# Expert tiles: the first product in three pieces of 512 columns instead of four of 384, and one of two projection pieces' rests made on GpSimd

## The chip, the cores and the metric

The kernel runs on one core of one Trainium2 chip. A core has a matrix engine (TensorE, PE), a vector engine (VectorE, DVE), a scalar engine (ScalarE, ACT), GpSimd (POOL) and a DMA-issuing engine (SyncE, SP), each with its own instruction queue; they meet through semaphores. The metric is the device time of one execution in microseconds, as the median of several executions.

## What is computed

A two-layer perceiver block over 16 x 64 tokens of width 512: cosine attention to a context, self-attention, a mixture of experts, cross-attention, a decayed attention and a feed-forward layer. The change is in the mixture of experts alone:

```python
scores = jax.nn.softmax(xf @ w_gate, axis=-1)
weights, idx = jax.lax.top_k(scores, TOP_K)            # 2 of 8 experts a token
...
h = jnp.einsum('ecd,edf->ecf', exp_x, c_fc)            # 512 -> 1536
a, g = jnp.split(h, 2, axis=-1)
h = jax.nn.silu(a) * g                                 # 768
exp_out = jnp.einsum('ecf,efd->ecd', h, c_proj)        # 768 -> 512
```

## The kernel before

`expert_layer` first routes: each of the 1024 tokens goes to two experts, the routed tokens are padded per expert to tiles of 128, and there are always ET = 23 such tiles. Then come 23 steps, one for each tile, written by `steps` as steps 0 and 1, a hardware loop over pairs of steps, and step 22.

Products are made of split operands, because TensorE multiplies the short type fp32r: each operand is a first part, which ScalarE makes by a copy into fp32r, and a rest, which VectorE makes by subtracting the first part from the whole (`rest`, L1049). Three products stand for one (first by first, first by rest, rest by first). Weights are split again for every tile: `fw` holds the two parts of the 512 x 1536 first weights, `pw` those of the 768 x 512 projection, each in one buffer only. `raw_fc` and `raw_pj` hold the whole weights of two experts; SyncE reloads one when the last tile that needs it has been split.

The order of the work is written out by hand, one function `step` for each engine, and each engine takes its instructions strictly in that order:

- TensorE (L950): `hidden(s, 0)` and `hidden(s, 1)` (12 matmuls of 384 columns each, into PSUM banks 0 and 1, the half under the silu), `turn_h(s - 1)` (6 transposes of the gated hidden values), `hidden(s, 2)` and `hidden(s, 3)` (the other half), `turn_x(s + 1)` (4 transposes of the next tile), `out_proj(s - 1)` (18 matmuls of 512 columns). `hidden(s, c)` waits for both parts of the tile (`x_lo`), for both parts of piece c of the weights (`fc_lo`), and until its bank was read.
- ScalarE (L1005): takes the result of two steps ago (`y_take`), then the first part of projection half 0, `silu(s, 0)`, `first_fc(s + 1, 0)`, `silu(s, 1)`, first parts of the turned hidden values (`first_h`, twice), of projection half 1, of piece 1 of the next tile's weights, of the next tile (`first_x`), of pieces 2 and 3. Ahead of `first_pj(s - 1, 0)` and of `first_fc(s + 1, 0)` its sequencer loads two values from memory (`parity_of`, `loaded`), which tell where the expert's weights lie and whether they have landed.
- VectorE (L1077): rest of projection half 0, of piece 0 of the next weights, of the turned hidden values (twice), of projection half 1; the gate product `product(s, 0)`, rest of piece 1, `product(s, 1)`, rest of the next tile (`rest_x`), rests of pieces 2 and 3.
- GpSimd (L1122): only issues DMAs: a tile's load, and the store of the tile two behind.

`first_fc(s + 1, c)` may not write `fw` before `hidden(s, c)` has read it:

```python
if not is_(s, 0):
    act.wait_ge(f_mm, BASE + 4 * s + c - 3)
nc.scalar.activation(fw[0][:, :, fc_cols(c)], raw_fc_of(par, c), ACT.Copy).then_inc(fc_hi, 1)
```

## Time and profile before

| | us |
|---|---|
| median of 3 runs | 2177.83 (2176.89 to 2182.11) |
| the profiled execution's own time | 2178.88 |
| its span from first to last instruction | 2177.1 |
| expert steps 1 to 21 in it, from the first matmul of step 1 to that of step 22 | 286.34 |

The span is a serial chain of six layers; the expert steps are its stretch from about 394 to 720 us. A row of the timeline gives start and duration in us, engine, line, operation, and in brackets how long the engine had been idle and what ended that. PE is TensorE's matmuls; L109 is the helper that issues split products; L1049 is the helper that makes rests.

### The profile page before, as it was taken

The page shows a single profiled execution, that of the slowest core. Times are in us where ns is not written, and L with a number is a line of the kernel's source. Part 1 is how long each engine was busy: PE and PEld are TensorE (multiplying, and loading weights), DVE is VectorE, ACT ScalarE, POOL GpSimd, SP SyncE. Part 2 cuts the span into 40 slices and gives each one's busy share as a digit, 9 for nine tenths or more (in the row PEclk, how much of TensorE's full clock was granted, in tenths as well). Part 3 has the DMA queues.
Part 4 walks back from the last instruction along what each step waited for, and adds up shares of the span by engine and source line. Part 5 has one row for each costly group of instructions (what it writes and reads, how often), then busy time and mean ns, then how long its engine had stood idle before and what let it go on. Part 6 is the DMA issues. An engine that isn't in the chain of part 4 may idle for free. (4 is left out here: it accounts for less than half of the span.)

```text
span 2177.1 us, 31504 instructions
## 1 busy us (share of the span) xinstructions
PE 1943.0 (89%) x10442; PEld 1494.0 (69%) x10442; DVE 1338.7 (61%) x2423; ACT 1120.6 (51%) x1846; POOL 125.4 (6%) x159
## 2 busy tenths in 40 slices
PE   7978983699999499999999999999968989858998
PEld 5647873699999477777777777787747666623443
DVE  5765662699998264536362635354448999839851
ACT  5753320688887244535353535444436666626640
POOL 0000002100000110000000000000000000012220
PEclk9989885899999799999999999999988888779999
DMA  7410005235332421001000101012040000020000
GB/s 262 147 54 1 0 0 222 112 131 205 130 150 89 153 68 49 34 29 34 29 34 29 48 14 48 14 48 92 1 171 1 1 1 1 1 82 0 5 10 25
DMA packets 25896, 137.45 MB, mean 63 GB/s; under 512 B 4066, under 2 KB 4194, under 8 KB 22116
## 3 DMA queue, kind: packets, MB, share of 16 engines
q1 hardware_dynamic: 19588, 116.18, 14.6%
q0 software_dynamic: 6240, 20.45, 2.8%
q8 instruction: 32, 0.52, 0.1%
q14 instruction: 36, 0.29, 0.0%
HBM read 116.17 MB, written 20.45 MB: 63 GB/s over the span
## 5 line engine op out<-in xcount | busy, mean ns | idle before, releaser
L109 PE MATMUL PS<-cT,qs 128*128 128x512 f32 x1152 | 295.6, 402 | 9.0 <-ACT pb L1406 7.0
L109 PE MATMUL PS<-pT,cN 128*128 128x512 f32 x1152 | 270.0, 392 | 1.7 <-DVE pT L1501 1.7
L109 PEld LDWEIGHTS PS<-cT,qs 128*128 128x128 f32 x1152 | 209.3, 189 | 59.9 <-issue 15.1
L109 PEld LDWEIGHTS PS<-pT,cN 128*128 128x128 f32 x1152 | 213.9, 188 | 45.3 <-DVE pT L1501 1.9
L109 PE MATMUL PS<-fw,xgT 128*128 128x384 f32 x1104 | 204.0, 339 | 3.0 <-DVE xgT L1049 3.0
L109 PEld LDWEIGHTS PS<-fw,xgT 128*128 128x128 f32 x1104 | 191.6, 189 | 8.3 <-issue 3.9
L109 PE MATMUL PS<-ws,xT 128*128 128x512 f32 x672 | 182.3, 430 | 6.4 <-DVE ws L563 4.9
L1049 DVE TENSOR_TENSOR fw<-W,fw 128x1536 fp32r<-128x1536 f32 x92 | 159.4, 1755 | 44.9 <-ACT fw L972 44.9
L1496 DVE TENSOR_REDUCE nmax<-PS 128x1 f32<-128x512 f32 x128 | 87.7, 685 | 156.9 <-PE PS L109 156.3
L109 PEld LDWEIGHTS PS<-ws,xT 128*128 128x128 f32 x672 | 138.8, 209 | 46.4 <-issue 11.3
L972 ACT ACTIVATE fw<-W 128x1536 fp32r x92 | 134.2, 1485 | 50.3 <-issue 50.3
L1401 ACT ACTIVATE qp<-PS 128x512 f32<-128x512 f32 x96 | 57.4, 598 | 189.6 <-PE PS L109 189.6
L2109 PE MATMUL PS<-xT,W 128*128 128x512 f32 x256 | 118.8, 614 | 1.3 <-ACT xT L2145 0.8
L1501 DVE TENSOR_TENSOR pT<-PS,pT 128x512 fp32r<-128x512 f32 x128 | 87.0, 685 | 52.9 <-ACT pT L1423 52.9
L2119 PE MATMUL PS<-W,hs 128*128 128x512 f32 x256 | 112.5, 592 | 0.0
L1423 ACT ACTIVATE pT<-PS 128x512 fp32r<-128x512 f32 x128 | 75.7, 598 | 65.4 <-PE PS L1301 65.2
L946 PE MATMUL PS<-pw,hT 128*128 128x512 f32 x414 | 101.8, 400 | 4.7 <-DVE hT L1049 4.7
L1406 ACT ACTIVATE pb<-PS,nmax 128x512 f32<-128x512 f32 x128 | 87.6, 685 | 34.5 <-DVE nmax L1496 34.4
L155 PE MATMUL PS<-cn,xn 128*128 128x128 f32 x160 | 29.0, 311 | 84.6 <-DVE xn L148 75.6
L1713 PEld LDWEIGHTS PS<-cn,W 128*128 128x128 f32 x512 | 78.0, 225 | 37.2 <-DVE W L2025 29.4
L142 POOL TENSOR_TENSOR rs<-ve,cn 128x1 f32<-128x1 f32 x41 | 23.4, 571 | 1390.2 <-DVE ve L137 1390.2
L1713 PE MATMUL PS<-cn,W 128*128 128x16 f32 x512 | 76.9, 285 | 22.5 <-DVE W L2025 22.4
(246 smaller groups left out, 3407.9 us busy)
## 6 DMA issues: line engine op xcount, KB each, us to landing
W<-in_fc SPq DMA_DIRECT2D x8, 3072.0 KB
cT<-in_ctxT SPq DMA_DIRECT2D x16, 768.0 KB, 5.4
raw_pj<-in_proj SPq DMA_DIRECT2D x8, 1536.0 KB, 6.4
ct_in<-in_ctxT SPq DMA_DIRECT2D x16, 768.0 KB
cn_in<-in_ctxN SPq DMA_DIRECT2D x16, 768.0 KB
W<-in_w SPq DMA_DIRECT2D x2, 4096.0 KB, 13.1
routed_x<-zero SPq DMA_DIRECT2D x23, 256.0 KB, 5.4
xg<-routed_x POOLq DMA_DIRECT2D x23, 256.0 KB, 3.2
```

The lines of the kernel that those rows point to most:

```text
L109: mm = nc.tensor.matmul(out, lhs(m, s), rhs(n, s), start=(opens and (s, m, n) == terms[0]), stop=((s, m, n) == terms[-1]))
L946: mm = nc.tensor.matmul(ps[7], hT[m][:, f, :], pw[n][:, f, :], start=(f == 0 and m == n), stop=(f == FK - 1 and m == 1))
L972: nc.scalar.activation(fw[0][:, :, fc_cols(c)], raw_fc_of(par, c), ACT.Copy).then_inc(fc_hi, 1)
L1049: return nc.vector.tensor_tensor(out, whole, first.bitcast(F32), ALU.subtract)
L1401: nc.scalar.activation(out, src, ACT.Copy, scale=scale).then_inc(w_sb, count)
L1406: nc.scalar.activation(pb[:, g % 2, :], ps[g % 2], ACT.Exp, bias=nmax[:, g % 4:g % 4 + 1], accum_out=rsum[:, g % 4:g % 4 + 1]).then_inc(e_ ...
L1423: nc.scalar.activation(turned(pT[0], g), ps[2 + g % 2].rearrange("p (j n) -> p j n", j=JK), ACT.Copy).then_inc(pt_hi, 1)
L1496: nc.vector.tensor_reduce(nmax[:, g % 4:g % 4 + 1], ps[g % 2], AX.X, ALU.max, negate=True).then_inc(m_dve, 1)
L1501: return nc.vector.tensor_tensor(out, whole, first.bitcast(F32), ALU.subtract)
L1713: mm = nc.tensor.matmul(ps[6 + c % 2][:, col:col + B], rb[:, t % RB, k * P:(k + 1) * P], sel, start=True, stop=True)
L2109: mm = nc.tensor.matmul(ps[n % HB], w16[:, k, f * P:(f + 1) * P], xT[g][:, k, :], start=(k == 0), stop=(k == DK - 1))
L2119: mm = nc.tensor.matmul(ps[HB + t % ZB], hs[:, t // TG, f, (t % TG) * P:(t % TG + 1) * P], w26[:, f, :], start=(f == 0), stop=(f == FT - 1))
```

## The change

The first product is cut into three pieces of 512 columns (12 matmuls each) instead of four of 384. Piece 0 holds columns 0 to 511 of the silu half; piece 1 holds its last 256 columns and the first 256 of the other half; piece 2 the remaining 512. So `silu` works on 512 and then 256 columns, and `product` on 256 and then 512, both after both silus. The rest of projection half 0 moves from VectorE to GpSimd, which gets its own semaphore for it, and stands there between the store of one tile and the load of a later one. VectorE's load of the parity for half 1 moves to just ahead of it.

```diff
@@ -669,7 +669,8 @@
         xg_in = [sem("xg_in3_0", pool_dma=True), sem("xg_in3_1", pool_dma=True)]
         y_out = [sem("y_out3_0", pool_dma=True), sem("y_out3_1", pool_dma=True)]
         x_mm, x_hi, x_lo = sem("x_mm3"), sem("x_hi3"), sem("x_lo3")
-        fc_hi, fc_lo, pj_hi, pj_lo = sem("fc_hi3"), sem("fc_lo3"), sem("pj_hi3"), sem("pj_lo3")
+        fc_hi, fc_lo, pj_hi = sem("fc_hi3"), sem("fc_lo3"), sem("pj_hi3")
+        pj_lo = [sem("pj_lo3_0"), sem("pj_lo3_1")]
         f_mm, silu_sb, hid_sb = sem("f_mm3"), sem("silu_sb3"), sem("hid_sb3")
         hT_mm, hT_hi, hT_lo = sem("hT_mm3"), sem("hT_hi3"), sem("hT_lo3")
         y_mm, y_sb = sem("y_mm3"), sem("y_sb3")
@@ -871,7 +872,9 @@
             return isinstance(s, int) and s == n
 
         def fc_cols(c):
-            return slice(c * HFE, (c + 1) * HFE)
+            return slice(c * 512, (c + 1) * 512)
+
+        MIX = 1024 - FE
 
         def pj_rows(g):
             return slice(g * HF, (g + 1) * HF)
@@ -895,14 +898,15 @@
                     end = sp.value_load(edge[0:1, ex - 2:ex - 1], min_val=0, max_val=ET)
                     u = ex % 2
                     sp.wait_ge(s_fc, BASE + 16 * ex)
-                    sp.wait_ge(fc_lo, end * 4 + BASE)
+                    sp.wait_ge(fc_lo, end * 3 + BASE)
                     sp.dma_start(raw_fc[:, u], a["fc"][ex]).then_inc(s_fc, 16)
                     sp.wait_ge(s_pj, BASE + 16 * ex)
-                    sp.wait_ge(pj_lo, end * 2 + BASE)
+                    for g in range(2):
+                        sp.wait_ge(pj_lo[g], end + BASE)
                     sp.dma_start(raw_pj[:, u], a["proj"][ex]).then_inc(s_pj, 16)
                 sp.wait_ge(s_fc, BASE + 16 * NE)
                 sp.wait_ge(s_pj, BASE + 16 * NE)
-                sp.wait_ge(fc_lo, BASE + 4 * ET)
+                sp.wait_ge(fc_lo, BASE + 3 * ET)
                 for dst, name in ((e.wq4, "wq4"), (e.wk4, "wk4"), (e.wv4, "wv4"), (e.wo4, "wo4")):
                     sp.dma_start(dst, a[name]).then_inc(e.s_w4, 16)
 
@@ -919,17 +923,20 @@
                 def hidden(s, c):
 
                     pe.wait_ge(x_lo, BASE + s + 1)
-                    pe.wait_ge(fc_lo, BASE + 4 * s + c + 1)
+                    pe.wait_ge(fc_lo, BASE + 3 * s + c + 1)
                     if not is_(s, 0):
-                        pe.wait_ge(silu_sb if c < 2 else hid_sb, BASE + 2 * s + c % 2 - 1)
-                    split_product(nc, ps[c][:, 0:HFE], lambda part, k: xgT[part][:, k, :],
+                        if c < 2:
+                            pe.wait_ge(silu_sb, BASE + 2 * s + c - 1)
+                        if c:
+                            pe.wait_ge(hid_sb, BASE + 2 * s + c - 2)
+                    split_product(nc, ps[c], lambda part, k: xgT[part][:, k, :],
                                   lambda part, k: fw[part][:, k, fc_cols(c)], DK).then_inc(f_mm, 1)
 
                 def turn_h(s):
 
                     pe.wait_ge(hT_lo, BASE + 2 * s)
+                    pe.wait_ge(hid_sb, BASE + 2 * s + 2)
                     for g in range(2):
-                        pe.wait_ge(hid_sb, BASE + 2 * s + g + 1)
                         for f in range(HF):
                             tr = nc.tensor.transpose(ps[5 + g][:, f * P:(f + 1) * P],
                                                      hid[:, (g * HF + f) * P:(g * HF + f + 1) * P], ident)
@@ -940,7 +947,7 @@
                     pe.wait_ge(y_sb, BASE + s)
                     for g in range(2):
                         pe.wait_ge(hT_lo, BASE + 2 * s + g + 1)
-                        pe.wait_ge(pj_lo, BASE + 2 * s + g + 1)
+                        pe.wait_ge(pj_lo[g], BASE + s + 1)
                         for f in range(g * HF, (g + 1) * HF):
                             for m, n in ((0, 0), (0, 1), (1, 0)):
                                 mm = nc.tensor.matmul(ps[7], hT[m][:, f, :], pw[n][:, f, :],
@@ -953,7 +960,6 @@
                     if not is_(s, 0):
                         turn_h(s - 1)
                     hidden(s, 2)
-                    hidden(s, 3)
                     if not is_(s, ET - 1):
                         turn_x(s + 1, 1 - u, pair + u)
                     if not is_(s, 0):
@@ -968,7 +974,7 @@
             def _(act):
                 def first_fc(s, c, par):
                     if not is_(s, 0):
-                        act.wait_ge(f_mm, BASE + 4 * s + c - 3)
+                        act.wait_ge(f_mm, BASE + 3 * s + c - 2)
                     nc.scalar.activation(fw[0][:, :, fc_cols(c)], raw_fc_of(par, c), ACT.Copy).then_inc(fc_hi, 1)
 
                 def first_pj(s, g, par):
@@ -981,14 +987,15 @@
 
                 def first_x(s):
                     act.wait_ge(x_mm, BASE + s + 1)
-                    act.wait_ge(f_mm, BASE + 4 * s)
+                    act.wait_ge(f_mm, BASE + 3 * s)
                     nc.scalar.activation(xgT[0][:, :, :].rearrange("p k t -> p (k t)"), ps[4], ACT.Copy).then_inc(x_hi, 1)
 
                 def silu(s, c):
-                    act.wait_ge(f_mm, BASE + 4 * s + c + 1)
+                    act.wait_ge(f_mm, BASE + 3 * s + c + 1)
                     if not is_(s, 0):
-                        act.wait_ge(hid_sb, BASE + 2 * s + c - 1)
-                    nc.scalar.activation(gated[:, fc_cols(c)], ps[c][:, 0:HFE], ACT.Silu).then_inc(silu_sb, 1)
+                        act.wait_ge(hid_sb, BASE + 2 * s)
+                    n = FE - 512 if c else 512
+                    nc.scalar.activation(gated[:, c * 512:c * 512 + n], ps[c][:, 0:n], ACT.Silu).then_inc(silu_sb, 1)
 
                 def first_h(s, g):
                     act.wait_ge(hT_mm, BASE + 2 * s + g + 1)
@@ -1024,13 +1031,12 @@
                         first_fc(s + 1, 1, par)
                         first_x(s + 1)
                         first_fc(s + 1, 2, par)
-                        first_fc(s + 1, 3, par)
 
                 par = parity_of(act, 0)
                 loaded(0, s_fc)
                 first_fc(0, 0, par)
                 first_x(0)
-                for c in range(1, 4):
+                for c in range(1, 3):
                     first_fc(0, c, par)
                 steps(act, step)
                 y_take(ET - 2, 1, (ET - 2) // 2)
@@ -1049,12 +1055,12 @@
                     return nc.vector.tensor_tensor(out, whole, first.bitcast(F32), ALU.subtract)
 
                 def rest_fc(s, c, par):
-                    ve.wait_ge(fc_hi, BASE + 4 * s + c + 1)
+                    ve.wait_ge(fc_hi, BASE + 3 * s + c + 1)
                     rest(fw[1][:, :, fc_cols(c)], raw_fc_of(par, c), fw[0][:, :, fc_cols(c)]).then_inc(fc_lo, 1)
 
                 def rest_pj(s, g, par):
                     ve.wait_ge(pj_hi, BASE + 2 * s + g + 1)
-                    rest(pw[1][:, pj_rows(g), :], raw_pj_of(par, g), pw[0][:, pj_rows(g), :]).then_inc(pj_lo, 1)
+                    rest(pw[1][:, pj_rows(g), :], raw_pj_of(par, g), pw[0][:, pj_rows(g), :]).then_inc(pj_lo[g], 1)
 
                 def rest_x(s):
                     ve.wait_ge(x_hi, BASE + s + 1)
@@ -1067,25 +1073,23 @@
                     rest(lo, ps[5 + g][:, 0:HF * P], hi).then_inc(hT_lo, 1)
 
                 def product(s, c):
-                    ve.wait_ge(silu_sb, BASE + 2 * s + c + 1)
-                    ve.wait_ge(f_mm, BASE + 4 * s + c + 3)
+                    ve.wait_ge(silu_sb, BASE + 2 * s + 2)
+                    ve.wait_ge(f_mm, BASE + 3 * s + c + 2)
                     if not is_(s, 0):
-                        ve.wait_ge(hT_mm, BASE + 2 * s + c - 1)
-                    nc.vector.tensor_tensor(hid[:, fc_cols(c)], gated[:, fc_cols(c)], ps[2 + c][:, 0:HFE],
-                                            ALU.mult).then_inc(hid_sb, 1)
+                        ve.wait_ge(hT_mm, BASE + 2 * s)
+                    cols = slice(MIX, FE) if c else slice(0, MIX)
+                    gate_in = ps[2] if c else ps[1][:, 512 - MIX:512]
+                    nc.vector.tensor_tensor(hid[:, cols], gated[:, cols], gate_in, ALU.mult).then_inc(hid_sb, 1)
 
                 def step(s, u, pair):
                     first, last = is_(s, 0), is_(s, ET - 1)
-                    if not first:
-                        par_p = parity_of(ve, s - 1)
-                        rest_pj(s - 1, 0, par_p)
                     if not last:
                         par = parity_of(ve, s + 1)
                         rest_fc(s + 1, 0, par)
                     if not first:
                         rest_h(s - 1, 0)
                         rest_h(s - 1, 1)
-                        rest_pj(s - 1, 1, par_p)
+                        rest_pj(s - 1, 1, parity_of(ve, s - 1))
                     product(s, 0)
                     if not last:
                         rest_fc(s + 1, 1, par)
@@ -1093,16 +1097,14 @@
                     if not last:
                         rest_x(s + 1)
                         rest_fc(s + 1, 2, par)
-                        rest_fc(s + 1, 3, par)
 
                 par = parity_of(ve, 0)
                 rest_fc(0, 0, par)
                 rest_x(0)
-                for c in range(1, 4):
+                for c in range(1, 3):
                     rest_fc(0, c, par)
                 steps(ve, step)
                 par = parity_of(ve, ET - 1)
-                rest_pj(ET - 1, 0, par)
                 rest_h(ET - 1, 0)
                 rest_h(ET - 1, 1)
                 rest_pj(ET - 1, 1, par)
@@ -1119,13 +1121,24 @@
                     pool.wait_ge(y_sb, BASE + s + 1)
                     nc.gpsimd.dma_start(yg_d[s * P:(s + 1) * P, :], y[:, s % 2, :]).then_inc(y_out[s % 2], 16)
 
+                def rest_pj(s):
+
+                    par = parity_of(pool, s)
+                    pool.wait_ge(pj_hi, BASE + 2 * s + 1)
+                    nc.gpsimd.tensor_tensor(pw[1][:, pj_rows(0), :], raw_pj_of(par, 0),
+                                            pw[0][:, pj_rows(0), :].bitcast(F32), ALU.subtract).then_inc(pj_lo[0], 1)
+
                 for s in range(ET):
                     if s >= 2:
                         pool.wait_ge(x_mm, BASE + s - 1)
                     nc.gpsimd.dma_start(xg[:, s % 2, :], xg_d[s * P:(s + 1) * P, :]).then_inc(xg_in[s % 2], 16)
+                    if s >= 3:
+                        store(s - 3)
                     if s >= 2:
-                        store(s - 2)
-                store(ET - 2)
+                        rest_pj(s - 2)
+                for s in range(ET - 3, ET - 1):
+                    store(s)
+                    rest_pj(s + 1)
                 store(ET - 1)
                 for u in range(2):
                     pool.wait_ge(y_out[u], 16 * ((ET + 1 - u) // 2))
```

On VectorE the two listings below show step 1, the second tile: from the rest of projection half 0 (`pw`, before) or of piece 0 of the next weights (`fw`, after) on. `fw` are rests of weight pieces, `hT` of turned hidden values, `pw` of projection halves, `hid` gate products, `xgT` the rest of the next tile; TENSOR_LOAD reads the parity. Before:

```order
L1049 ISA
L1049 TENSOR_TENSOR pw<-raw_pj,pw 128x1536
L889 TENSOR_LOAD parity
L889 ISA x2
L1049 ISA
L1049 TENSOR_TENSOR fw<-W,fw 128x4x384
L1049 TENSOR_TENSOR hT<-PS,hT 128x384 x2
L1049 ISA
L1049 TENSOR_TENSOR pw<-raw_pj,pw 128x1536
L1074 TENSOR_TENSOR hid<-gated,PS 128x384
L1049 ISA
L1049 TENSOR_TENSOR fw<-W,fw 128x4x384
```

After, the same step:

```order
L1055 TENSOR_TENSOR fw<-W,fw 128x4x512
L1055 TENSOR_TENSOR hT<-PS,hT 128x384 x2
L892 TENSOR_LOAD parity
L892 ISA x2
L1055 ISA
L1055 TENSOR_TENSOR pw<-raw_pj,pw 128x1536
L1082 TENSOR_TENSOR hid<-gated,PS 128x256
L1055 ISA
L1055 TENSOR_TENSOR fw<-W,fw 128x4x512
L1082 TENSOR_TENSOR hid<-gated,PS 128x512
L1055 TENSOR_TENSOR xgT<-PS,xgT 128x512
```

The first `pw` is gone from the head of the step; all that followed it keeps its order, with pieces of 4 x 512 in place of 4 x 384.

On GpSimd the listings show the stretch after the first three tile loads (`xg<-routed_x`). Before:

```order
L1125 DMA xg<-routed_x 128x512 x3
L1120 DMA routed_y<-y 128x512
L1125 DMA xg<-routed_x 128x512
L1120 DMA routed_y<-y 128x512
L1125 DMA xg<-routed_x 128x512
```

After:

```order
L1134 DMA xg<-routed_x 128x512 x3
L892 TENSOR_LOAD parity
L892 ISA x2
L1128 ISA
L1128 TENSOR_TENSOR pw<-raw_pj,pw 128x1536
L1134 DMA xg<-routed_x 128x512
L1122 DMA routed_y<-y 128x512
L892 TENSOR_LOAD parity
L892 ISA x2
L1128 ISA
L1128 TENSOR_TENSOR pw<-raw_pj,pw 128x1536
L1134 DMA xg<-routed_x 128x512
```

A subtraction (`pw`) stands ahead of every later tile load, and each store (`routed_y`) comes one tile load later than before.

## Rows read from the trace of the kernel before

**Rows 1.** The page: busy time of each engine over the whole span.
```profile
PE 1943.0 (89%) x10442; PEld 1494.0 (69%) x10442; DVE 1338.7 (61%) x2423; ACT 1120.6 (51%) x1846; POOL 125.4 (6%) x159
```

**Rows 2.** Windows, expert tiles 1 to 21: length, busy of each engine, granted clock, DMA.
```profile
core 0: us, PE busy (x) PEld busy (x) DVE busy (x) ACT busy (x) POOL busy (x), PEclk, DMA share, GB/s
409.27:695.61 286.34, 286.32 (x1596) 266.49 (x1597) 265.76 (x232) 236.20 (x253) 21.46 (x40) 1.00 0.37 136
```

**Rows 3.** Timeline of one tile, step 11: start, duration, engine, line, op, idle before.
```profile
559.34 4.43 PE L109 MATMUL PS<-fw,xgT 128*128 128x384 f32 x24
559.58 0.60 ACT L1003 ACTIVATE y<-PS 128x512 f32<-128x512 f32 x1 [0.77 <-PE PS L946]
...
561.05 1.49 ACT L976 ACTIVATE pw<-raw_pj 128x1536 fp32r x1 [0.87 <-issue]
562.45 0.47 ACT L991 ACTIVATE gated<-PS 128x384 f32<-128x384 f32 x1
562.69 1.76 DVE L1049 TENSOR_TENSOR pw<-raw_pj,pw 128x1536 fp32r<-128x1536 f32 x1 [0.25 <-ACT pw L976]
563.42 1.49 ACT L972 ACTIVATE fw<-W 128x1536 fp32r x1 [0.51 <-issue]
...
565.05 1.76 DVE L1049 TENSOR_TENSOR fw<-W,fw 128x1536 fp32r<-128x1536 f32 x1 [0.61 <-ACT fw L972]
...
566.73 1.01 DVE L1049 TENSOR_TENSOR hT<-PS,hT 128x384 fp32r<-128x384 f32 x2
...
567.66 1.75 DVE L1049 TENSOR_TENSOR pw<-raw_pj,pw 128x1536 fp32r<-128x1536 f32 x1
...
568.78 4.36 PE L946 MATMUL PS<-pw,hT 128*128 128x512 f32 x18
...
569.33 0.55 DVE L1074 TENSOR_TENSOR hid<-gated,PS 128x384 f32<-128x384 f32 x1
...
569.79 1.75 DVE L1049 TENSOR_TENSOR fw<-W,fw 128x1536 fp32r<-128x1536 f32 x1
571.46 0.55 DVE L1074 TENSOR_TENSOR hid<-gated,PS 128x384 f32<-128x384 f32 x1
571.92 0.68 DVE L1049 TENSOR_TENSOR xgT<-PS,xgT 128x512 fp32r<-128x512 f32 x1
...
572.98 1.23 PE L109 MATMUL PS<-fw,xgT 128*128 128x384 f32 x6
```

**Rows 4.** Groups by line, other shapes: count, busy, mean ns of one, idle before.
```profile
L597 DVE TENSOR_TENSOR sc<-PS,mx 128x256 f32<-128x256 f32 x32 | 11.3, 417 | 0.9
...
L1875 DVE TENSOR_TENSOR ws<-W,ws 128x2048 fp32r<-128x2048 f32 x4 | 9.0, 2289 | 6.2 <-ACT ws L1773 6.2
...
L1773 ACT ACTIVATE ws<-W 128x2048 fp32r<-128x2048 f32 x4 | 7.4, 1902 | 12.1 <-PEq L2298 12.1
```

**Rows 5.** Groups by line on GpSimd, the same columns.
```profile
L2090 POOL TENSOR_TENSOR dg<-g 128x512 f32<-128x512 f32 x32 | 41.5, 1296 | 124.1 <-ACT g L2171 124.1
...
L447 POOL MEMSET pf<- 128x2048 f32 x1 | 1.8, 1805 | 30.2 <-POOLq L2298 30.2
```

**Rows 6.** Timeline of the feed-forward stage, GpSimd beside VectorE.
```profile
1962.98 1.32 POOL L2090 TENSOR_TENSOR dg<-g 128x512 f32<-128x512 f32 x1 [2.82 <-ACT g L2171]
...
1963.20 1.65 DVE L2214 SCALAR_TENSOR_TENSOR hs<-y,up 128x512 f32<-128x512 f32 x1
...
1967.61 0.69 DVE L2214 SCALAR_TENSOR_TENSOR hs<-y,up 128x512 f32<-128x512 f32 x1
```

**Rows 7.** Timeline of the expert stage's first and last step.
```profile
396.93 10.31 PE L109 MATMUL PS<-fw,xgT 128*128 128x384 f32 x48 [1.41 <-DVE xgT L1049]
...
402.63 1.49 ACT L972 ACTIVATE fw<-W 128x1536 fp32r x1 [0.55 <-issue]
...
710.27 1.48 ACT L976 ACTIVATE pw<-raw_pj 128x1536 fp32r x1 [0.72 <-issue]
...
714.22 5.97 PE L946 MATMUL PS<-pw,hT 128*128 128x512 f32 x18 [4.66 <-DVE hT L1049]
```

## Prediction, made before the changed kernel ran

> **What bounds the kernel now.** I read the page first. TensorE is busy 89% of the span [rows 1], which says little, since the page is an average over six layers and only one is changed. So I took the windows of the expert steps next. From the first matmul of step 1 to that of step 22 there are 21 periods in 286.34 us, 13.635 us each, and TensorE is busy for all but 0.02 us of them, at a granted clock of 1.00 (the 2.4 GHz level) [rows 2]. VectorE is busy 265.76 us, 93%, ScalarE 82%. TensorE sets the period, and VectorE is close behind.
>
> How close is in the timeline of one tile, and there the reader should follow the hand-over rather than the busy shares [rows 3]. TensorE starts a tile at 559.34 and the next at 572.98. That next start also needs the rest of the next tile, which VectorE ends at 571.92 + 0.68 = 572.60. Behind that end stands a chain that began with this very tile: its first piece of products, on ScalarE silu (562.45) and the first part of the next weights' piece 0 (563.42), then on VectorE without a gap the rest of that piece (565.05), two rests of turned values (566.73), projection half 1 (567.66), gate product (569.33), rest of piece 1 (569.79), gate product (571.46), rest of the tile (571.92). The loop closes once a tile and has only 0.38 us to spare. Whatever lengthens it by more sets the period instead of TensorE.
>
> **TensorE's own work.** The 18 projection matmuls of 512 columns read 4.36 us, and 24 of 384 columns read 4.43 [rows 3]: 0.242 and 0.185 us each. Thirty-six of the wide kind are 8.72 us, 48 of the narrow 8.86. Time goes by columns, and both cuts have 18,432 columns; TensorE gains 0.14 us a tile, 3 us over the stage, if it stays the bound.
>
> **VectorE's work.** It loses one rest of 1.76 us. Its rest of a piece goes from 1.755 to 2.289 us (the same form at 128 x 2048 in another layer, [rows 4]), three of them 6.87 against four 7.02. The two gate products go from 0.55 twice to 0.42 [rows 4] and 0.69 (the 512-column rest of the tile, [rows 3]). Sum: about 1.9 us less a tile. On shares this looks like relief. But the removed rest (562.69 to 564.45) is not in the chain: VectorE waited 0.61 us behind it for ScalarE's piece 0 [rows 3]. Its removal only lengthens a wait. It costs nothing there and gives nothing.
>
> **The chain with the new pieces**, counted from TensorE's start of a tile:
>
> 1. Piece 0: 12 of 18 times 4.36 is 2.91 us; with the drain of the last matmul and the signal I take 3.1 (before, with 384 columns, some 2.4).
> 2. ScalarE's silu can start at 3.1. Before, it waited for projection half 0 on its own engine until 562.45, which is also 3.1; that cover of the shorter piece is gone, since the projection half will end near 2.0 (below).
> 3. The two loads before the next `fw`. After `y_take` (559.58) the engine's next work started at 561.05, 1.47 us after its start, though it was done after 0.60; the rest is called issue [rows 3]. The same two loads stand behind silu. There the gap was 563.42 - 562.45 = 0.97 us, because the sequencer had begun while silu still queued behind the projection half. Now silu does not queue. I take 1.47; bounds are 0.97 and 1.7 (the same loads counted from when piece 0 was ready, 561.7, by the 2.4 above). Piece 0's first part starts at 4.57.
> 4. First part of 128 x 2048: 1.90 us [rows 4], and 0.14 to VectorE (563.42 + 1.49 to 565.05): 6.61.
> 5. VectorE start to start, from the starts in [rows 3]: rest of piece 0 1.68 + 0.53 = 2.21; two turned rests 0.93; projection half 1 1.67; gate product of 256 columns 0.46 - 0.13 = 0.33; rest of piece 1 1.67 + 0.53 = 2.20; gate product of 512 columns 0.46 + 0.14 = 0.60; rest of the tile 0.68. Together 8.62 against 7.55 before. The moved parity load runs ahead on the sequencer under the rest of piece 0: nothing; without that cover 0.5 us.
> 6. 0.05 us of signal to TensorE: 15.28 us.
>
> The period becomes 15.28 instead of 13.635, 1.64 us more, 21 times: 34.5 us. TensorE then waits some 1.8 us a tile for `x_lo`, and VectorE idles from about 2.2 to 6.6 us of each period. Piece 1's and piece 2's banks and weights are ready well before: the chain alone decides. `out_proj` starts with the turned rests at about 9.85 instead of 9.4 and ends near 14.2, within the slack.
>
> **GpSimd.** It has no subtraction of this size in the trace. Nearest is 128 x 512 in 1.296 us [rows 5]. Three times 1.296 is 3.9; the bound below is VectorE's 1.76. I take 3.7. The projection half's first part ends near 2.0 of the period (`y_take` at 14.3 of the tile before, 1.47 for the loads, 1.5 for itself), VectorE's rest of piece 2 near 2.2. Does it hinder VectorE? A feed-forward row shows that it can: a VectorE instruction of two SBUF inputs that began at 1963.20, inside GpSimd's subtraction of 1962.98 to 1964.30, took 1.65 us; its like without company 0.69 [rows 6]. The overlap, 1.10 us, was nearly lost whole (0.96). So the rest of piece 2 goes first, GpSimd runs from 2.2 to 5.9, and VectorE next wants such an instruction at 6.6: free, with 0.7 to spare. The projection needs the result at 9.85: covered by 3.9 us.
>
> The Trainium skill, "SBUF — State Buffer", section "Who interferes with whom", calls this an exclusive lock: a VectorE instruction with two SBUF inputs and a GpSimd instruction that reads SBUF block each other for a whole instruction. By that rule, the trace agrees (1.65 against 0.69). By itself it speaks against moving such work to GpSimd at all; if all of it fell beside VectorE's rests the sum would be that of the second rival below. The same notes' "GPSIMD Engine Reference", section 3.1, has 4497 ns for 2048 columns; an estimate from that page is 3.4 us for 1536, and the sum would not move.
>
> **Start and end.** Step 0: its 48 products took 10.31 us [rows 7], 1.45 over twice 4.43; if all of that fell on piece 0 it took 3.7, and a third more columns cost up to 1.2; I take 0.9; then first part +0.41, VectorE +1.07 (two rests and two gate products): 2.4 us later at step 1. Last step: the final projection started at 714.22 [rows 7]. Now it waits for GpSimd, from ScalarE's end at 711.75 plus 0.15 plus 3.7: 715.6, 1.4 us later. Step 22 itself is as TensorE sets it.
>
> **Sum.** 34.5 + 2.4 + 1.4 = 38.3 us on the profiled execution's 2178.88, which lies 1.05 above the median: 2177.83 + 38.3 = 2216.1.
>
> **Rivals.**
>
> - *TensorE stays the bound* (not slower). For it: TensorE is never idle now, and VectorE is given 1.9 us less. It needs the chain of 15.28 to be under 13.5, so 1.8 us of it must overlap in a way the order of the queues forbids. Time: -3 + 2.4 + 1.4, 2178.6.
> - *The lock adds to VectorE throughout.* VectorE's 12.66 us a tile (265.76 / 21) less 1.9 plus 3.7 of blocking is 14.46 us, 0.83 over the period of now. If the chain were somehow not closed, 0.83 x 21 + 3.8: 2199.0. Against it: GpSimd's turn falls into VectorE's idle stretch.
> - *GpSimd longer than 4.4 us.* Then it reaches past 6.6 and every further microsecond lengthens every period. At 5.5 us: 1.1 x 21 + 1.8 at the end above the forecast, 2241.
> - *The clock falls* from TensorE's waits. Against it: TensorE waited 1.60 us ahead of step 1 and then ran 24 in 4.44 us [rows 7], as later, at a granted 1.00 [rows 2]. If the level of 1.2 GHz held for piece 0 of each tile, +3 us a tile: 2279.
>
> **Chances and range.** Forecast 0.80; TensorE bound 0.05; lock throughout 0.05; long GpSimd 0.06; clock 0.02; anything else 0.02. Inside the forecast, the loads at 0.97 give -10.5 (2205.6), at 1.7 give +4.8 (2220.9); cover lost for the parity load adds 10 more. So 2203 to 2231. No change means within 0.3%, 6.5 us, about what a measurement of this kernel tells apart. Faster 0.01, within 0.3% 0.05, slower 0.94.
>
> **What would show it.** A period of 15.1 to 15.5 us between first matmuls; TensorE waiting 1.5 to 2 us in front of L109, released by VectorE's `xgT`; VectorE idle 4 to 5 us before its rest of piece 0, released by ScalarE's `fw`; ScalarE's `fw` 1.4 to 1.6 us after the start of the 512-column silu; 36 wide matmuls at 0.23 to 0.25 each; GpSimd's subtraction at 3.4 to 3.9 us, over before VectorE's rest of piece 0 begins. The forecast is wrong if TensorE shows no wait, if a rest on VectorE reads longer than 2.3 us beside GpSimd, or if the loads hide under silu.

## The result, and the profile after

The changed kernel takes 2223.31 us (median of 4 runs, 2219.84 to 2227.95) against 2178.24 of the kernel before, 45.1 us more: a ratio of 1.0205, 95% interval 1.0182 to 1.0229. The profiled execution's own time is 2227.95, its span 2225.8, so it lies 4.6 above the median; that of before was 0.6 above.

First the windows, the same reading as [rows 2], from the first matmul of step 2 to that of step 22:

```profile
core 0: us, PE busy (x) PEld busy (x) DVE busy (x) ACT busy (x) POOL busy (x), PEclk, DMA share, GB/s
430.24:741.01 310.77, 280.56 (x1281) 220.22 (x1281) 216.23 (x181) 221.92 (x220) 93.19 (x60) 1.00 0.33 124
```

Twenty periods in 310.77 us are 15.54 each; before, 13.635. TensorE is busy 280.56 us of them, 90%; before it read busy throughout. VectorE falls from 93% to 70%. No engine is full now, and every one of the twenty periods has nearly the same length (15.52 to 15.60 us): a chain through several engines that closes once a period would look like this. The experiments below test it. The clock is 1.00 in both.

The timeline of step 11 answers to [rows 3]. (Rows: start, duration, engine, line, operation, idle time before and what ended it. Lines moved: L1055 makes rests, L978 first parts of weights, L998 the silu, L1082 the gate product, L1128 GpSimd's rest.)

```profile
570.17 5.73 PE L109 MATMUL PS<-fw,xgT 128*128 128x512 f32 x24 [1.52 <-DVE xgT L1055]
571.82 3.69 POOL L1128 TENSOR_TENSOR pw<-raw_pj,pw 128x1536 fp32r<-128x1536 f32 x1 [1.69 <-ACT pw L982]
573.30 0.60 ACT L998 ACTIVATE gated<-PS 128x512 f32<-128x512 f32 x1 [1.66 <-PE PS L109]
574.80 1.92 ACT L978 ACTIVATE fw<-W 128x2048 fp32r x1 [0.90 <-issue]
...
576.86 2.29 DVE L1055 TENSOR_TENSOR fw<-W,fw 128x2048 fp32r<-128x2048 f32 x1 [4.73 <-ACT fw L978]
...
579.07 1.01 DVE L1055 TENSOR_TENSOR hT<-PS,hT 128x384 fp32r<-128x384 f32 x2
...
580.00 1.75 DVE L1055 TENSOR_TENSOR pw<-raw_pj,pw 128x1536 fp32r<-128x1536 f32 x1
...
581.67 0.41 DVE L1082 TENSOR_TENSOR hid<-gated,PS 128x256 f32<-128x256 f32 x1
...
582.00 2.29 DVE L1055 TENSOR_TENSOR fw<-W,fw 128x2048 fp32r<-128x2048 f32 x1
584.20 0.68 DVE L1082 TENSOR_TENSOR hid<-gated,PS 128x512 f32<-128x512 f32 x1
...
584.80 0.68 DVE L1055 TENSOR_TENSOR xgT<-PS,xgT 128x512 fp32r<-128x512 f32 x1
...
585.72 5.75 PE L109 MATMUL PS<-fw,xgT 128*128 128x512 f32 x24 [1.52 <-DVE xgT L1055]
```

Read it from TensorE's start at 570.17. The silu starts at 573.30, 3.13 later (forecast 3.1). The next piece's first part starts 1.50 behind the silu's start, of which 0.90 the engine did nothing (forecast 1.47). VectorE starts the rest of it at 576.86, 2.06 later (2.04), after 4.73 us of idling, and ends the rest of the tile at 584.80 + 0.68 = 585.48, 8.62 later (8.62). TensorE starts at 585.72 (it had waited 1.52), 0.24 behind (0.05). GpSimd's 3.69 us end at 575.51, 1.35 ahead of VectorE's start. Everything stands within 0.03 us of the forecast but the last hop.

No piece of work in these rows was slower than priced: 24 wide matmuls took 5.73 us, 0.239 each (forecast 0.242), and a rest of 2048 columns 2.29.

**Where the 48.7 us between the two spans are.** All from the starts of step 0, 1, 2 and 22 on TensorE and of the first routed sum on VectorE:

| stretch | before | after | difference | forecast |
|---|---|---|---|---|
| up to step 0 | 396.93 | 398.03 | 1.1 | 0 |
| step 0 | 12.34 | 14.43 | 2.1 | 2.4 |
| step 1 | 13.65 | 17.78 | 4.1 | 1.6 |
| steps 2 to 21 | 272.69 | 310.77 | 38.1 | 32.9 |
| step 22 to the routed sum | 32.94 | 35.13 | 2.2 | 1.4 |
| all behind | 1448.5 | 1449.7 | 1.1 | 0 |

The first and last rows are layers that the change does not touch; across the profiles of this study the last one read 1445.7 to 1451.8, so they are scatter.

Step 1 has a cost of its own. The prediction set the clock rival aside by the wait ahead of this step; the row, which [rows 7] does not hold, is this one of the kernel before:

```profile
409.27 4.44 PE L109 MATMUL PS<-fw,xgT 128*128 128x384 f32 x24 [1.60 <-DVE xgT L1049]
```

After, the same place reads:

```profile
412.46 8.61 PE L109 MATMUL PS<-fw,xgT 128*128 128x512 f32 x24 [3.92 <-DVE xgT L1055]
412.55 5.38 POOL L1128 TENSOR_TENSOR pw<-raw_pj,pw 128x1536 fp32r<-128x1536 f32 x1 [15.09 <-ACT pw L982]
...
417.98 0.60 ACT L998 ACTIVATE gated<-PS 128x512 f32<-128x512 f32 x1 [5.64 <-PE PS L109]
```

TensorE waited 3.92 us instead of 1.60, and then 24 wide products took 8.61 us instead of 5.73. The granted clock in windows around it (PEclk stands behind POOL's count):

```profile
core 0: us, PE busy (x) PEld busy (x) DVE busy (x) ACT busy (x) POOL busy (x), PEclk, DMA share, GB/s
408.00:412.00 4.00, 0.54 (x5) 0.30 (x3) 4.00 (x5) 3.73 (x4) 0.00 (x0) 0.97 0.00 0
412.00:414.00 2.00, 1.54 (x4) 1.25 (x5) 2.00 (x2) 0.35 (x1) 1.45 (x1) 0.50 0.00 0
418.00:420.00 2.00, 2.00 (x8) 1.55 (x8) 0.00 (x0) 1.27 (x2) 0.42 (x1) 0.85 0.37 104
420.00:424.00 4.00, 4.00 (x22) 3.39 (x21) 2.63 (x2) 4.00 (x6) 0.00 (x0) 1.00 0.03 13
```

It falls to 0.50, the lower level of 1.2 GHz, at the end of the wait, is 0.50 when step 1 starts, and is 1.00 again by 420. In the later steps, with waits of 1.5 us, it stays at 1.00. Step 1 is 2.2 us longer than the steps after it, and the links say where: the silu starts 5.52 us behind TensorE's start (417.98 - 412.46) instead of 3.13, because the twelve products of piece 0 ran at the lower level, and all links behind it together are as in step 11 within 0.2 us. GpSimd's 5.38 us beside it are not the cause: pieces_alone, without them, has the same step 1.

At the end the final projection now waits for GpSimd:

```profile
757.29 3.43 POOL L1128 TENSOR_TENSOR pw<-raw_pj,pw 128x1536 fp32r<-128x1536 f32 x1 [1.55 <-ACT pw L982]
757.53 1.02 DVE L1055 TENSOR_TENSOR hT<-PS,hT 128x384 fp32r<-128x384 f32 x2 [5.32 <-ACT hT L1003]
...
759.40 2.93 DVE L1055 TENSOR_TENSOR pw<-raw_pj,pw 128x1536 fp32r<-128x1536 f32 x1 [0.85 <-ACT pw L982]
...
760.87 7.11 PE L953 MATMUL PS<-pw,hT 128*128 128x512 f32 x18 [5.95 <-POOL pw L1128]
```

It starts 19.86 us behind step 22's start (760.87 - 741.01); before 18.61 (714.22 - 695.61). And it takes 7.11 us instead of 5.97 [rows 7], behind a wait of 5.95 instead of 4.66. The granted clock was 0.50 in the first 3.1 us of it; before, it was 0.61 and 0.53 in the first two stretches of 2 us. VectorE's last projection rest reads 2.93 instead of 1.76: it began inside GpSimd's. The two turned rests that VectorE made inside the same GpSimd instruction were not held up: they read one input from PSUM (`hT<-PS,hT`), and took 1.02 us against 1.01 before.

### The profile page after: what moved, and what is told of

The parts are those of the page before. It is cut to its first block and busy times, and to the rows that moved or that the text cites. A ratio compares the mean times of both kernels' runs of the same rounds, so it can differ in the third digit from the quotient of the medians.

```text
span 2225.8 us, 30866 instructions
## 1 busy us (share of the span) xinstructions
PE 1954.3 (88%) x10166; PEld 1458.0 (66%) x10166; DVE 1298.0 (58%) x2377; ACT 1118.4 (50%) x1823; POOL 210.0 (9%) x182
## 5 line engine op out<-in xcount | busy, mean ns | idle before, releaser
L109 PE MATMUL PS<-cT,qs 128*128 128x512 f32 x1152 | 295.3, 402 | 9.0 <-ACT pb L1419 7.0
L109 PE MATMUL PS<-pT,cN 128*128 128x512 f32 x1152 | 270.4, 392 | 1.7 <-DVE pT L1514 1.7
L109 PEld LDWEIGHTS PS<-cT,qs 128*128 128x128 f32 x1152 | 209.0, 189 | 59.8 <-issue 15.1
L109 PEld LDWEIGHTS PS<-pT,cN 128*128 128x128 f32 x1152 | 214.0, 188 | 45.5 <-DVE pT L1514 1.9
L109 PE MATMUL PS<-fw,xgT 128*128 128x512 f32 x828 | 205.2, 402 | 36.8 <-DVE xgT L1055 36.8
L1055 DVE TENSOR_TENSOR fw<-W,fw 128x2048 fp32r<-128x2048 f32 x69 | 157.7, 2287 | 133.0 <-ACT fw L978 133.0
L109 PEld LDWEIGHTS PS<-fw,xgT 128*128 128x128 f32 x828 | 155.3, 192 | 77.6 <-issue 38.5
L109 PE MATMUL PS<-ws,xT 128*128 128x512 f32 x672 | 181.1, 428 | 6.4 <-DVE ws L563 4.9
L109 PEld LDWEIGHTS PS<-ws,xT 128*128 128x128 f32 x672 | 138.0, 208 | 45.9 <-issue 11.3
L978 ACT ACTIVATE fw<-W 128x2048 fp32r x69 | 132.5, 1921 | 56.8 <-issue 56.8
```

What stands on the lines that cost most here:

```text
L109: mm = nc.tensor.matmul(out, lhs(m, s), rhs(n, s), start=(opens and (s, m, n) == terms[0]), stop=((s, m, n) == terms[-1]))
L1055: return nc.vector.tensor_tensor(out, whole, first.bitcast(F32), ALU.subtract)
```

## Experiments

Periods below are read as above, from step 2's start to step 22's, divided by 20.

| kernel | ratio to before, 95% interval | period | step 1 | from step 22 |
|---|---|---|---|---|
| before | | 13.635 | 13.65 | 32.94 |
| changed | 1.0205 (1.0182 to 1.0229) | 15.54 | 17.78 | 35.13 |
| pieces_alone | 1.0193 (1.0168 to 1.0218) | 15.53 | 17.78 | 32.89 |
| gpsimd_alone | 1.0069 (1.0042 to 1.0096) | 14.11 | 15.01 | 35.12 |
| loads_early | 1.0125 (1.0100 to 1.0149) | 14.62 | 17.07 | 34.78 |
| gpsimd_twice | one run, 2286.5 us | 18.07 | 17.80 | 40.54 |
| tile_rest_early | 1.0067 (1.0052 to 1.0083) | 14.05 | 17.34 | 34.55 |
| x_wait_last | 1.0204 (1.0188 to 1.0219) | 15.38 | 17.56 | 35.15 |
| all_three_vector | 0.9986 (0.9975 to 0.9996) | 13.45 | 13.60 | 33.10 |
| all_three_gpsimd | 1.0066 (1.0051 to 1.0082) | 14.05 | 17.25 | 34.46 |
| tile_rest_early_vector | 1.0019 (1.0009 to 1.0028) | 13.75 | 13.70 | 33.54 |
| four_pieces_same_edits | 1.0003 (0.9994 to 1.0013) | 13.56 | 13.64 | 33.89 |

**pieces_alone**: GpSimd's part undone.

```diff
+                    if not first:
+                        par_p = parity_of(ve, s - 1)
+                        rest_pj(s - 1, 0, par_p)
                     if not last:
                         par = parity_of(ve, s + 1)
                         rest_fc(s + 1, 0, par)
...
```

(`rest_pj(ET - 1, 0, par)` is back behind the steps too, and GpSimd only issues DMAs again.)

> Three pieces of 512 columns, the rest of projection half 0 back on VectorE at the head of its step. Chain theory (ScalarE piece 0, VectorE from the rest of piece 0 to the rest of the tile): that rest falls into VectorE's idle stretch of 4.7 us and costs nothing, so the period stays 15.5 us and TensorE still waits 1.5 us a tile for xgT; about 2221, at most 2 us off the changed kernel, with a last step 1.5 to 3 us shorter. Rival, GpSimd's turn beside VectorE (the lock) costs: period back towards 13.6 to 14.5, below 2200. Rival, VectorE's total work sets the period: it grows by 1.7 us to 17.3, 2260.

```profile
572.19 1.75 DVE L1055 TENSOR_TENSOR pw<-raw_pj,pw 128x1536 fp32r<-128x1536 f32 x1
...
576.98 2.29 DVE L1055 TENSOR_TENSOR fw<-W,fw 128x2048 fp32r<-128x2048 f32 x1 [3.03 <-ACT fw L978]
```

The period is the same to 0.01 us, with 1.75 us more on VectorE in each: the rest falls into its idle stretch, which shrinks from 4.73 to 3.03 us. Total work is not the bound. The whole loss of the steady steps comes from the wide pieces; moving the rest brought nothing in them and cost 2.2 us in the last step.

**gpsimd_alone**: the four pieces of before, GpSimd's part kept.

```diff
-                    if not first:
-                        par_p = parity_of(ve, s - 1)
-                        rest_pj(s - 1, 0, par_p)
...
+                    if s >= 2:
+                        rest_pj(s - 2)
```

> Four pieces of 384 columns as before, only the rest of projection half 0 moved to GpSimd. Chain theory with the lock: GpSimd starts near 3.2 us of the period and runs to 6.8, VectorE wants the rest of piece 0 at 5.6, waits 1.1 us, and the chain, which had 0.38 us to spare, sets a period of 14.3 to 14.5 instead of 13.64: about 2194 to 2198, and VectorE's rest of piece 0 reads near 2.9 us instead of 1.76. If the lock did not hold: period 13.64, 2180 (the last step 1.5 us longer), all VectorE rests at 1.76.

Slower by 0.7%: 16.3 us in the medians (2191.73 against 2175.44), of which 9.5 are twenty periods of 0.47 more, 1.4 step 1 and 2.2 the end; the rest, some 3 us, is no more than the scatter between executions. The timeline of one step:

```profile
569.87 3.52 POOL L1124 TENSOR_TENSOR pw<-raw_pj,pw 128x1536 fp32r<-128x1536 f32 x1 [1.69 <-ACT pw L978]
...
572.51 2.50 DVE L1051 TENSOR_TENSOR fw<-W,fw 128x1536 fp32r<-128x1536 f32 x1 [2.49 <-ACT fw L974]
...
580.13 0.68 DVE L1051 TENSOR_TENSOR xgT<-PS,xgT 128x512 fp32r<-128x512 f32 x1
...
581.04 4.43 PE L109 MATMUL PS<-fw,xgT 128*128 128x384 f32 x24 [0.30 <-DVE xgT L1051]
```

VectorE's rest of piece 0 began at 572.51 while GpSimd's ran until 573.39, and took 2.50 us instead of 1.75; TensorE, idle for 0.3 us, starts 0.23 behind the rest of the tile. The overlap of 0.88 us cost 0.75. The loop of [rows 3] is 13.26 us long there (559.34 to 572.60), 13.50 with a hop of 0.24. Here VectorE's rest of piece 0 starts 0.13 us earlier behind TensorE's start (566.93) and takes 0.75 longer: 14.12, and the period is 14.11. The forecast had an overlap of 1.1 us, a period of 14.3 to 14.5 and 2194 to 2198 us: the mechanism holds, the period was put too high by 0.2 to 0.4 us and the time by at least 2 us. By the Trainium skill, "SBUF — State Buffer", section "Who interferes with whom", the two instructions exclude each other for the whole instruction; the trace agrees to within 0.13 us.

**loads_early**: ScalarE's two loads ahead of the silu.

```diff
+                    if not last:
+                        par = parity_of(act, s + 1)
+                        loaded(s + 1, s_fc)
                     silu(s, 0)
                     if not last:
-                        par = parity_of(act, s + 1)
-                        loaded(s + 1, s_fc)
                         first_fc(s + 1, 0, par)
```

> The changed kernel with ScalarE's two loads for the next piece 0 placed ahead of silu(s, 0) instead of behind it. Chain theory: the first part of piece 0 starts 0.6 us after the silu's start instead of 1.50, all later links move up by 0.9; the period falls from 15.54 to 14.5 to 14.8 (the higher value if GpSimd's rest then reaches past the start of VectorE's rest of piece 0, which should read up to 0.2 us longer): 2202 to 2207. If something other than this chain sets the period (wide products, the clock, bank hand-over): 2223 as before.

```profile
590.65 0.60 ACT L998 ACTIVATE gated<-PS 128x512 f32<-128x512 f32 x1 [1.17 <-PE PS L109]
591.14 1.91 ACT L978 ACTIVATE fw<-W 128x2048 fp32r x1
```

The first part follows the silu's start by 0.49 us instead of 1.50, and the period fell by 0.92 to 14.62 (forecast 14.5 to 14.8). In every second step VectorE's rest of piece 0 reads 2.42 to 2.45 us instead of 2.29, for GpSimd's subtraction now reaches past its start. So these loads, which the profile shows only as idle time with the releaser "issue", were a full link of the chain.

**gpsimd_twice**: its subtraction made twice, the second behind a semaphore of the first.

```diff
+                    nc.gpsimd.tensor_tensor(pw[1][:, pj_rows(0), :], raw_pj_of(par, 0),
+                                            pw[0][:, pj_rows(0), :].bitcast(F32), ALU.subtract).then_inc(again, 1)
+                    pool.wait_ge(again, BASE + s + 1)
```

> The changed kernel with GpSimd's subtraction made twice, one behind the other (same result). GpSimd then works from 1.7 to some 9.2 us of the period. Lock theory: VectorE's rest of piece 0, wanted at 6.7, waits for the second one's end: it reads near 4.7 us instead of 2.29, the period grows by 2.3 to 2.6 to near 18.0, time near 2275. Without the lock: the projection needs it only at 9.5, so the period stays 15.5 and the time within 5 us of 2223.

```profile
580.81 3.52 POOL L1129 TENSOR_TENSOR pw<-raw_pj,pw 128x1536 fp32r<-128x1536 f32 x1 [1.68 <-ACT pw L983]
...
583.98 2.50 DVE L1056 TENSOR_TENSOR fw<-W,fw 128x2048 fp32r<-128x2048 f32 x1 [6.08 <-ACT fw L979]
...
584.41 5.38 POOL L1132 TENSOR_TENSOR pw<-raw_pj,pw 128x1536 fp32r<-128x1536 f32 x1
...
587.34 4.07 DVE L1056 TENSOR_TENSOR pw<-raw_pj,pw 128x1536 fp32r<-128x1536 f32 x1
...
589.84 5.99 PE L954 MATMUL PS<-pw,hT 128*128 128x512 f32 x18 [2.94 <-POOL pw L1132]
...
608.10 4.34 PE L954 MATMUL PS<-pw,hT 128*128 128x512 f32 x18 [2.99 <-POOL pw L1132]
```

The period is as forecast, 18.07 to 18.0, but by another way than was written down. VectorE's rest of piece 0 slipped in between the two subtractions (2.50 us, not 4.7) and the second waited behind it (5.38 us). VectorE's rest of projection half 1 then waited in turn (4.07), and TensorE waited 2.94 us for GpSimd's result at the projection. The exclusion is shown in both directions. The period holds a third thing too: in 12 of the twenty steps the 18 projection matmuls behind such a wait took 5.97 to 7.09 us, as at 589.84, in the other 8 they took 4.33 to 4.47, as at 608.10, and the granted clock over the twenty periods is 0.93 instead of 1.00. How much of the 2.5 us is the clock's and how much the exclusion's was not taken apart. A period of 18.0 alone would have been taken for proof of a path that was not there.

**tile_rest_early**: VectorE's rest of the tile ahead of the rest of piece 1.

```diff
                     product(s, 0)
                     if not last:
+                        rest_x(s + 1)
                         rest_fc(s + 1, 1, par)
                     product(s, 1)
                     if not last:
-                        rest_x(s + 1)
                         rest_fc(s + 1, 2, par)
```

> The changed kernel with VectorE's rest of the next tile placed ahead of the rest of piece 1 instead of behind the second gate product. Chain theory: the chain from the silu to that rest loses the rest of piece 1 and the second gate product (2.8 us), so it no longer sets the period; but VectorE's queue then ends later against TensorE's start, GpSimd's subtraction begins only behind the rest of piece 2 (near 4 us) and holds VectorE's rest of piece 0 up: period 14.1 to 14.5, 2192 to 2202. Without the lock it would be TensorE's 13.5, 2180.

```profile
582.32 5.61 PE L109 MATMUL PS<-fw,xgT 128*128 128x512 f32 x24
```

1.49 us off the period by one exchange; from step 2 on TensorE waits nowhere ahead of L109 any more. At 14.05 the period lies just under the range forecast. It is still above 13.5, and all_three_gpsimd below shows why.

**x_wait_last**: TensorE's wait for the tile behind its other waits.

```diff
-                    pe.wait_ge(x_lo, BASE + s + 1)
                     pe.wait_ge(fc_lo, BASE + 3 * s + c + 1)
...
+                    pe.wait_ge(x_lo, BASE + s + 1)
```

> The changed kernel with TensorE's wait for the rest of the tile as the last of its waits ahead of a piece, so that the register arithmetic for the other waits lies in front of it. The hop from VectorE's end to TensorE's first matmul should fall from 0.24 to 0.05 us in the loop steps, the period from 15.54 to 15.35, the time by 3 to 4 us to 2219. If the 0.24 us is the signal itself: no change.

```profile
599.55 0.68 DVE L1055 TENSOR_TENSOR xgT<-PS,xgT 128x512 fp32r<-128x512 f32 x1
...
600.29 5.74 PE L109 MATMUL PS<-fw,xgT 128*128 128x512 f32 x24 [1.31 <-DVE xgT L1055]
```

The hop is 600.29 - 600.23, 0.06 us, and the period fell by 0.15 (forecast 0.19). Three microseconds in all are below what the runs tell apart (a ratio of 1.0204 to before, against 1.0205 of the changed kernel); here the trace settles it.

**all_three_vector**: the three edits (diffs of loads_early, tile_rest_early, x_wait_last) together, and that of pieces_alone.

> Three pieces of 512, all rests on VectorE, ScalarE's loads ahead of the silu, the tile's rest ahead of the rest of piece 1, TensorE's tile wait last. Chain theory: TensorE is the bound again, never waits in steps 2 to 21, and the period is what 36 wide products give: 13.45 to 13.55, 0.1 to 0.2 us below the kernel before; with a start some 1 to 2 us later, 2174 to 2179. If wide products themselves were slower: period above 13.64.

```profile
571.56 5.61 PE L109 MATMUL PS<-fw,xgT 128*128 128x512 f32 x24
...
574.99 0.60 ACT L998 ACTIVATE gated<-PS 128x512 f32<-128x512 f32 x1 [0.27 <-issue]
...
575.48 1.91 ACT L978 ACTIVATE fw<-W 128x2048 fp32r x1
...
577.54 2.29 DVE L1056 TENSOR_TENSOR fw<-W,fw 128x2048 fp32r<-128x2048 f32 x1 [0.69 <-ACT fw L978]
...
585.00 5.60 PE L109 MATMUL PS<-fw,xgT 128*128 128x512 f32 x24
```

TensorE goes from 571.56 to 585.00 without a wait. It is 0.14% faster than the kernel before (interval 0.04% to 0.25%): 2172.63 against 2176.78 us in the runs that stood beside each other. That beats both kernels, but the gain over the kernel before is so small that the interval only just leaves out no change.

**all_three_gpsimd**: the three edits without that of pieces_alone, so GpSimd makes the rest.

> The same with the rest of projection half 0 on GpSimd. Lock theory: GpSimd's 3.6 us now fall beside VectorE's rest of piece 0, which reads up to 1.5 us longer; period 13.9 to 14.5, 2188 to 2200. If moving the rest relieved VectorE without a price: 13.5 and 2178.

```profile
584.24 3.65 POOL L1129 TENSOR_TENSOR pw<-raw_pj,pw 128x1536 fp32r<-128x1536 f32 x1 [1.71 <-ACT pw L982]
...
586.85 3.19 DVE L1056 TENSOR_TENSOR fw<-W,fw 128x2048 fp32r<-128x2048 f32 x1 [2.33 <-ACT fw L978]
...
590.56 4.54 PE L953 MATMUL PS<-pw,hT 128*128 128x512 f32 x18 [0.20 <-DVE hT L1056]
```

VectorE's rest of piece 0 reads 3.19 us instead of 2.29 and the projection waits 0.20 for the turned rests behind it. The move costs 0.60 us a tile here (14.05 against 13.45 of all_three_vector) and 3.7 us in step 1, once nothing else hides it. In step 1 VectorE's rest of piece 2, begun at 411.68, stands behind GpSimd's subtraction, begun at 411.63:

```profile
417.35 4.61 PE L109 MATMUL PS<-fw,xgT 128*128 128x512 f32 x12 [1.85 <-DVE fw L1056]
```

TensorE waits 1.85 us for it, and piece 2 then takes 4.61 us instead of 2.99; the granted clock was 0.50 from 418 to 420. tile_rest_early has the same long step 1.

**tile_rest_early_vector**: the diffs of tile_rest_early and of pieces_alone.

> Three pieces of 512, all rests on VectorE, and of the three edits only the tile's rest ahead of the rest of piece 1. Chain theory: taking the rest of piece 1 and the second gate product out of the chain suffices (2.8 us against the 1.9 by which it was too long), TensorE never waits from step 2 on, period 13.45 to 13.55, 2172 to 2178. If the loads or the wait's place still mattered: period 13.6 to 13.9.

The forecast missed: 13.75, not 13.45 to 13.55; 0.2% slower than before.

```profile
577.15 1.92 ACT L978 ACTIVATE fw<-W 128x2048 fp32r x1 [0.86 <-issue]
...
579.22 2.29 DVE L1055 TENSOR_TENSOR fw<-W,fw 128x2048 fp32r<-128x2048 f32 x1 [1.25 <-ACT fw L978]
...
581.42 1.01 DVE L1055 TENSOR_TENSOR hT<-PS,hT 128x384 fp32r<-128x384 f32 x2
581.49 0.60 PE L920 MATMUL PS<-cn,xg 128*128 128x128 f32 x4
...
582.03 4.54 PE L953 MATMUL PS<-pw,hT 128*128 128x512 f32 x18
```

With the loads still behind the silu, the rest of piece 0 starts at 579.22 and the first of the two turned rests, which is all that the first half of `out_proj` needs of them, ends at about 581.9 (half of 1.01 us behind 581.42, an estimate). TensorE began the transposes ahead of `out_proj` at 581.49 and `out_proj` 0.54 us later; in all_three_vector the same two starts are 0.35 us apart, so it is 0.2 us late. This reads as a second loop, from silu through the turned rests to the projection, which the first had hidden. That it and the place of TensorE's wait make up the whole 0.30 us by which the period exceeds all_three_vector's was not tried apart.

**four_pieces_same_edits**: the kernel before with the three edits; with four pieces the one on VectorE reads:

```diff
                     if not last:
+                        rest_x(s + 1)
                         rest_fc(s + 1, 1, par)
                     product(s, 1)
                     if not last:
-                        rest_x(s + 1)
                         rest_fc(s + 1, 2, par)
                         rest_fc(s + 1, 3, par)
```

> Control: the kernel before (four pieces of 384, all on VectorE) with the same three edits of order. TensorE was the bound there and stays it: period 13.60 to 13.65, time as before within 3 us. If the gain of the other version came from the order alone: 4 us faster here as well, period 13.45.

No change that can be measured in the time; the period is 0.08 us shorter, 13.56, and so just under the 13.60 to 13.65 forecast. So the kernel before did not run quite at TensorE's own pace. Its loop already held TensorE's start back in many steps:

```profile
558.42 0.69 DVE L1049 TENSOR_TENSOR xgT<-PS,xgT 128x512 fp32r<-128x512 f32 x1
```

That rest ends at 559.11 and TensorE starts the tile at 559.34 [rows 3], a hop of 0.23 to 0.24 us, the same as in the changed kernel. So it is at 11 of its 21 starts from step 2 to step 22. Against this version the wide pieces save 0.11 us a tile (13.56 to 13.45), 2 us in all: this is what the cut is worth by itself, where nothing else is in its way.

## Why the prediction was right

It forecast 2216 us, 2203 to 2231, and the time is 2223, with the cause that it named. Its sum of 38.3 us more stands against 45.1 in the medians; every term that was off was off in the same direction but step 0, so nothing large cancelled.

- *Wide pieces give TensorE next to nothing.* Forecast 0.14 us a tile; shown at 0.11 by the last two versions.
- *The removed rest was not in the chain.* Shown by pieces_alone.
- *The lengthened chain sets the period.* Each link was as forecast within 0.03 us but the last; the start of the projection, which is no link of the chain, was put at 9.85 us and came at 9.50 (579.67 - 570.17), at no cost. Cutting it at the loads, at the order on VectorE and at TensorE's wait took 0.92, 1.49 and 0.15 us off.
- *GpSimd blocks VectorE, but its turn falls into idle time.* Shown: no cost in the changed kernel's steady steps, 0.47 us a tile in gpsimd_alone. The rival in which it adds throughout was out by its place, not by its mechanism.
- *The term that was off most* is the hop to TensorE, 0.24 instead of 0.05 us, 4 us over the stage. 0.05 is what the start of step 1 shows (409.27), which stands outside the hardware loop; in the loop the kernel before has 0.24 in its own rows, at 559.34 for one. The spare time of 0.38 us, read at the start that follows (572.98), was therefore 0.14 there, and nothing at 11 of the 21 starts. (Counted from 0, the tile of [rows 3] is step 12 and not 11.) x_wait_last shows that the place of the wait makes the difference; that it is the register arithmetic of the waits behind it is read from the code. A further 1.5 us over the stage are the three links ahead of VectorE's, each 0.02 to 0.03 longer than forecast.
- *Step 1*: 2.2 us that were not in the sum. The clock rival was priced for all tiles and set aside by a wait of 1.60 us, but ahead of step 1 the wait grew to 3.92. The prediction had forecast step 1's later start, 2.4 us on top of 1.60, and did not ask what it does to TensorE's clock. For the later steps the rival was rightly set aside: 1.00 throughout.
- *The end*: 2.2 instead of 1.4. The start of the final projection moved by 1.25 as priced; the rest is its longer run, 7.11 us instead of 5.97, at a lower granted clock behind a longer wait.

## What to carry to other kernels

When an engine's busy share is near full and a second one is close behind, write down the loop from one iteration's start to the next, link by link, before counting work: a bigger piece lengthens each link that works on it, and work taken off an engine gives nothing unless it stood in that loop. The order inside a queue is worth more than its load: moving one 0.68 us instruction ahead of a 2.29 us and another 0.68 us one gave back 1.49 us of the 1.90 lost. Sequencer work (loads of values, register arithmetic) belongs ahead of the wait it would otherwise follow; look for idle time with the releaser "issue". When a trace shows how much time a loop has to spare, take the hop from the last semaphore to the next start off it, read inside the loop: 0.38 us were 0.14 here.

## What was not expected of the hardware

- A wait of 3.92 us of TensorE was followed by the clock's lower level until between 418 and 420 us, and 24 wide products took 8.61 us; waits of 1.5 us in twenty later steps were not. In between it went either way: of twenty waits of 2.0 to 3.0 us in gpsimd_twice, 12 were followed by projections of 5.97 to 7.09 us and 8 by ones of 4.33 to 4.47, and waits of 2.9 to 3.0 us stand on both sides.
- GpSimd's and VectorE's blocking is mutual: GpSimd's subtraction, 3.43 us at least, read 5.38 where VectorE was inside a rest of 2048 columns, and VectorE's 1.75 read 4.07 where GpSimd's was in front. The blocked instruction shows as a longer one, not as idle time. VectorE's rests with one input in PSUM were not lengthened inside GpSimd's (1.02 us against 1.01).
